# A vision tower on one core: attention four slots earlier, routing shared with GpSimd, and the chunk loop written out

## The reference, cut to what matters

```python
# 1: window attention, 8x8 windows, 8 heads of 8 channels, 2D rotary encoding
q, k, v = split(xw @ qkv_w.T + qkv_b);  q, k = rope2(q), rope2(k)
h = merge(softmax(q * 8**-0.5 @ k.T) @ v) @ proj_w.T + proj_b
# 2: mamba on layernorm(h), per image a scan over 4096 tokens
u = layernorm(h)
xb, z = split(rmsnorm(u) * norm_w @ in_proj_w.T)
xb = silu(causal_conv4(xb) + conv_b)                      # 128 channels
delta = softplus(xb @ projDelta_w.T + b);  B, C = xb @ projB_w.T, xb @ projC_w.T
state = exp(delta * A) * state + (xb * delta) * B         # 128 x 16 states
y = (sum(state * C) + xb * D) * silu(z)
h = h + y @ out_proj_w.T + u
# 3: experts on layernorm(h): 6 experts of three 64x64 layers, the best 2 of 6
p = softmax(relu(f @ rw1 + rb1) @ rw2 + rb2);  top2 = softmax(top_k(p, 2))
out = h + sum over top2 of weight * expert(f)
```

## Time and profile before

| | |
|---|---|
| median of 3 runs | 1921.03 us (1919.44 to 1929.98) |
| profiled execution | 1921.91 us, span 1920.1 us |
| PE busy | 1396.5 us (73%) |
| DVE busy | 1341.6 us (70%) |
| POOL busy | 1209.0 us (63%) |
| ACT busy | 1086.1 us (57%) |
| mean granted clock of TensorE | 0.806 |
| moved by DMA | 304.52 MB, mean 159 GB/s |
| first scan starts, last scan starts | 207.9 us, 1844.3 us |

### The profile page before, as it was taken

How to read it: one execution, slowest core, us unless ns; L and a number is a source line. 1 busy time by engine, 2 the same in 40 slices (tenths; PEclk the granted TensorE clock), 3 DMA queues, 4 the chain that set the end, 5 groups by cost and what they waited for, 6 DMA issues and landing times. The chain is left out here.

```text
span 1920.1 us, 31423 instructions
## 1 busy us (share of the span) xinstructions
PE 1396.5 (73%) x8148; PEld 648.9 (34%) x8148; DVE 1341.6 (70%) x1835; ACT 1086.1 (57%) x2020; POOL 1209.0 (63%) x1665
## 2 busy tenths in 40 slices
PE   3765768787969697786869687686868687666565
PEld 1443434343425243243424333242424333121111
DVE  1111688888786857878686867879686877878941
ACT  1234657675565747575475756566575857564432
POOL 2014486867685856767585765768586776967651
PEclk9877979796878878797788878796987978676755
DMA  2001686666565655666465665566566666777820
GB/s 63 1 14 57 162 226 192 195 187 173 159 200 156 182 167 157 189 186 173 138 185 174 165 190 162 174 169 193 150 170 184 172 198 175 213 192 204 222 70 6
DMA packets 214770, 304.52 MB, mean 159 GB/s; under 512 B 78924, under 2 KB 79128, under 8 KB 214424
## 3 DMA queue, kind: packets, MB, share of 16 engines
q1 hardware_dynamic: 214552, 302.09, 55.8%
HBM read 274.75 MB, written 20.97 MB: 154 GB/s over the span
## 5 line engine op out<-in xcount | busy, mean ns | idle before, releaser
L1262 POOL TENSOR_TENSOR hc<-hs,c_rep 128x512 f32<-128x512 f32 x512 | 652.2, 1274 | 461.0 <-DVE hs L1014 458.6
L1014 DVE TENSOR_TENSOR_SCAN hs<-bank,state,xd 128x512 f32<-128x512 f32 x512 | 650.8, 1273 | 83.2 <-issue 57.8
L767 ACT ACTIVATE bank<-dl,a_neg 128x512 f32<-128x512 f32 x512 | 350.3, 687 | 209.7 <-DVE hs L1014 186.7
L1005 DVE TENSOR_TENSOR xd<-xd,bank 128x512 f32<-128x512 f32 x512 | 337.1, 663 | 57.1 <-PE bank L439 53.3
L1032 DVE TENSOR_REDUCE neg_max<-bank 128x8 f32<-128x512 f32 x128 | 88.1, 688 | 281.1 <-PE bank L528 272.6
L538 PE MATMUL bank<-q_diag,k_heads 128*128 128x128 f32 x1024 | 226.4, 348 | 6.0 <-ACT shift L760 4.5
L538 PEld LDWEIGHTS bank<-q_diag,k_heads 128*128 128x128 f32 x1024 | 193.8, 229 | 82.8 <-issue 65.5
L775 ACT ACTIVATE probsT<-bank 128x512 f32<-128x512 f32 x128 | 76.4, 597 | 256.1 <-PE bank L539 255.6
L528 PE MATMUL bank<-k_heads,q_diag 128*128 128x512 f32 x256 | 175.1, 772 | 56.3 <-DMA q_diag<-rot 25.5
L449 PE MATMUL bank<-hc,wts 128*32 128x512 f32 x1024 | 182.8, 777 | 4.0 <-POOL hc L1262 2.6
L1334 POOL TENSOR_TENSOR ew<-ew,e 128x512 f32<-128x512 f32 x96 | 121.4, 1264 | 64.9 <-ACT e L760 64.8
(11 more groups left out here) (176 smaller groups left out, 2493.3 us busy)
## 6 DMA issues: line engine op xcount, KB each, us to landing
xd<-xdel_rows SPq DMA_DIRECT2D x512, 256.0 KB, 4.1
dl<-delta_rows SPq DMA_DIRECT2D x512, 256.0 KB, 3.8
delta_rows<-delta SPq DMA_DIRECT2D x16, 512.0 KB, 6.3
xdel_rows<-xdel SPq DMA_DIRECT2D x16, 512.0 KB, 3.1
xin<-in_x_dram SPq DMA_DIRECT2D x32, 128.0 KB, 2.4
q_diag<-rot SPq DMA_DIRECT2D x32, 128.0 KB
out_dram<-res SPq DMA_DIRECT2D x256, 16.0 KB
k_heads<-rot SPq DMA_DIRECT2D x128, 16.0 KB
```

What stands on the lines that cost most here:

```text
L767: act.activation(decay_ps[n % 2][:, :], dl[:, n % 4, :], ACT.Exp, scale=a_neg[:, g:g + 1])\
L1005: dve.tensor_tensor(xd[:, n % 8, :], xd[:, n % 8, :], b_ps[:, :], ALU.mult).then_inc(injected.sem, 1)
L1014: dve.tensor_tensor_scan(hs[:, n % 4, :], decay_ps[n % 2][:, :], xd[:, n % 8, :], state[:, g:g + 1], ALU.mult, ALU.add).then_inc(scanned.s ...
L1262: pool.tensor_tensor(hc[:, n % 8, :], hs[:, n % 4, :], c_rep[:, BAND * h:BAND * h + BAND], ALU.mult)\
```

## The change

`run` writes out all 21 bodies, and the counts become constants. Attention starts in slot 5 (`attention_at`), and `AT` gives the pairs 5, 6 and 7 three steps each; their maximum comes one step after their scores. What follows attention moves three slots ahead, as do SP's copies; the projection stands in slot 5 in a function of its own, and the sum of h and its layer norm moves from slot 6 of the next body to slot 17, in three buffers. `keys_queries` stands late in a slot. Of 26 routing steps 13 are on POOL, in slots 15 and 17 to 22, with DVE's in slots 15 and 17 to 22 and one memset dropped; the weights and all that follows move one slot back. `outT` shares its memory with `fT`. The matmuls of 8 columns are gone from `keys_queries` and `layer2`.

```diff
@@ -80,8 +80,8 @@
 
 
 
-AT = {"S": [9 + 2 * _w for _w in range(NW)], "max": [11 + 2 * _w for _w in range(NW)],
-      "T": [12 + 2 * _w for _w in range(NW)], "P": [13 + 2 * _w for _w in range(NW)]}
+AT = {"S": [9, 11, 13, 15, 17, 20, 23, 26], "max": [11, 13, 15, 17, 19, 21, 24, 27],
+      "T": [12, 14, 16, 18, 20, 23, 26, 29], "P": [13, 15, 17, 19, 21, 24, 27, 30]}
 
 
...
-        h_ln = sb("h_ln", [128, 2, NW, C])
+        h_ln = sb("h_ln", [128, 3, NW, C])
...
-        outT = sb("outT", [128, 512])
+
+        outT = fT
...
-        route_dve = sig("route_dve", 25)
+        route_dve = sig("route_dve", 12)
+        route_pool = sig("route_pool", 13)
...
@@ -284,18 +285,13 @@
         def attention_at(c, n):
 
 
-            return (c + 3, n - 9) if n >= 9 else (c + 2, n + 23)
+            return (c + 3, n - 5) if n >= 5 else (c + 2, n + 27)
 
         def run(eng, body):
 
 
 
-            for c in range(-3, 3):
-                body(c, c % 2)
-            with eng.Fori(3, NCH - 4, 2) as c:
-                body(c, 1)
-                body(c + 1, 0)
-            for c in range(NCH - 3, NCH + 2):
+            for c in range(-3, NCH + 2):
                 body(c, c % 2)
...
                     if has(c + 3):
-                        if n == 4:
+                        if n == 1:
                             load(c + 3)
-                        if 13 <= n < 15:
-                            heads(c + 3, 4 * (n - 13), 4 * (n - 12))
-                        if n == 14:
+                        if 10 <= n < 12:
+                            heads(c + 3, 4 * (n - 10), 4 * (n - 9))
+                        if n == 11:
                             queries(c + 3)
...
@@ -462,8 +458,6 @@
                     fill(use, k)
                 if names[0] == "k":
                     pe.wait_ge(A["xT"].drained, A["xT"].empty(k))
-
-                pe.matmul(uses[0].bank[0:32, 0:8], col("y_sel", 0, 32), xT[:, 0:8], start=True, stop=True)
                 for crossed, use in enumerate(uses):
                     for half in range(2):
                         p, to = slice(64 * half, 64 * half + 64), 64 * (half ^ crossed)
@@ -472,16 +466,16 @@
                     last.then_inc(use.filled, 1)
 
             def attend_first(k, s):
+                if s in AT["T"]:
+                    turned(k, AT["T"].index(s))
+                if s in AT["P"]:
+                    values(k, AT["P"].index(s))
+
+            def attend(k, s):
                 if s == 1:
                     keys_queries(k, ("k", "q"), ("wk", "wq"))
                 if s == 3:
                     keys_queries(k, ("k2", "q2"), ("wk2", "wq2"))
-                if s in AT["T"]:
-                    turned(k, AT["T"].index(s))
-                if s in AT["P"]:
-                    values(k, AT["P"].index(s))
-
-            def attend(k, s):
...
-                if s == 30:
+                if s == 31:
                     use = A["oT"]
                     fill(use, k)
                     pe.wait_ge(att_ready.sem, att_ready.at(k, 1))
...
-                if s == 31:
-                    use = A["proj"]
-                    fill(use, k)
+            def project(k):
+                use = A["proj"]
+                fill(use, k)
+                pe.wait_ge(A["oT"].drained, A["oT"].empty(k))
...
-                if n == 22:
+                if n == 23:
                     use = F["wT"]
                     fill(use, k)
-                    pe.wait_ge(route_dve.sem, route_dve.at(k, 25))
+                    pe.wait_ge(route_pool.sem, route_pool.at(k, 13))
...
-                if n == 25:
+                if n == 26:
                     use = F["outT"]
...
-                for e, slot in enumerate((27, 29, 31)):
+                for e, slot in enumerate((28, 30, 32)):
                     if n == slot:
                         layer3(k, e)
-                if n == SLOTS + 1:
+                if n == SLOTS + 2:
                     use = F["out"]
                     fill(use, k)
...
-                if 23 <= n < 23 + 2 * EP:
-                    j = PAIRED[n - 23]
+                if 24 <= n < 24 + 2 * EP:
+                    j = PAIRED[n - 24]
...
@@ -690,8 +684,6 @@
                 uses = F[f"h2_{e}"], G[f"h2_{e}"]
                 for use in uses:
                     fill(use, k)
-
-                pe.matmul(uses[0].bank[0:32, 0:8], col("y_sel", 0, 32), e1[:, 0, 0:8], start=True, stop=True)
...
@@ -722,6 +714,8 @@
                         spread_b(c + 1, 1 - odd, 0)
                     if has(k):
                         attend_first(k, s)
+                    if has(c + 2) and n == 5:
+                        project(c + 2)
...
-                if n == 15:
-                    act.wait_ge(route_dve.sem, route_dve.at(k, 3))
+                if n == 16:
+                    act.wait_ge(route_pool.sem, route_pool.at(k, 1))
                     act.activation(rt[:, 2, :, :], rt[:, 1, :, :], ACT.Exp).then_inc(route_act.sem, 1)
-                if n == 18:
-                    act.wait_ge(route_dve.sem, route_dve.at(k, 14))
+                if n == 21:
+                    act.wait_ge(route_pool.sem, route_pool.at(k, 6))
                     act.activation(st_f[:, 14, :], st_f[:, 13, :], ACT.Exp).then_inc(route_act.sem, 1)
...
-                if 24 <= n < 24 + 2 * EP:
-                    i = n - 24
+                if 25 <= n < 25 + 2 * EP:
+                    i = n - 25
...
-                if n == 22:
+                if n == 23:
                     use = F["wT"]
...
-                if n == SLOTS:
+                if n == SLOTS + 1:
                     use = F["outT"]
...
@@ -1033,7 +1027,7 @@
                                       X_AXIS, ALU.max, negate=True).then_inc(use.drained, 1)
 
             def attend(k, s):
...
-                if n == 9:
+                if n == 6:
                     use = A["proj"]
...
-                if n == 10:
+                if n == 7:
                     dve.wait_ge(A["proj"].drained, A["proj"].empty(k))
                     dve.tensor_reduce(st[:, 0, :], hid[:, :, :], X_AXIS, ALU.add).then_inc(done.sem, 1)
-                if n == 14:
+                if n == 11:
                     dve.wait_ge(ln1_act.sem, ln1_act.at(k, 1))
                     dve.tensor_reduce(st[:, 2, :], sq[:, :, :], X_AXIS, ALU.add).then_inc(done.sem, 1)
...
-                if 15 <= n < 20:
+                if 15 <= n < 23:
                     route(k, n)
...
@@ -1107,74 +1101,34 @@
             def route(k, n):
 
                 st, done = st_f, route_dve
+                def over(src, to, op):
+                    dve.tensor_reduce(st[:, to, :], rt[:, src, :, :], X_AXIS, op).then_inc(done.sem, 1)
+
                 if n == 15:
                     use = F["lg"]
                     dve.wait_ge(use.filled, use.full(k))
...
-                    dve.tensor_reduce(st[:, 10, :], rt[:, 0, :, :], X_AXIS, ALU.max).then_inc(done.sem, 1)
-                    dve.wait_ge(done.sem, done.at(k, 1))
-                    dve.tensor_tensor(rt[:, 1, :, :], rt[:, 0, :, :], wide_of(10), ALU.subtract).then_inc(done.sem, 1)
-                    dve.memset(rt[:, 12, :, :], 0.0).then_inc(done.sem, 1)
-                    dve.wait_ge(done.sem, done.at(k, 3))
-                if n == 16:
+                    over(0, 10, ALU.max)
+                if n == 17:
                     dve.wait_ge(route_act.sem, route_act.at(k, 1))
-                    dve.tensor_reduce(st[:, 11, :], rt[:, 2, :, :], X_AXIS, ALU.add).then_inc(done.sem, 1)
-                    dve.wait_ge(done.sem, done.at(k, 4))
+                    over(2, 11, ALU.add)
+                    dve.wait_ge(done.sem, done.at(k, 2))
                     dve.reciprocal(st[:, 12, :], st[:, 11, :]).then_inc(done.sem, 1)
-                    dve.wait_ge(done.sem, done.at(k, 5))
...
+
+                for i, (at, src, to, mask, count) in enumerate(((18, 3, 16, 4, 2), (19, 5, 10, 6, 3), (20, 7, 17, 8, 5),
+                                                                (21, 9, 10, 10, 7))):
+                    if n == at:
+                        dve.wait_ge(route_pool.sem, route_pool.at(k, count))
+                        over(src, to, ALU.max)
+                        dve.wait_ge(done.sem, done.at(k, 4 + 2 * i))
+                        dve.tensor_tensor(rt[:, mask, :, :], rt[:, src, :, :],
+                                          st[:, to, :].unsqueeze(2).to_broadcast([128, NW, E]), ALU.is_equal)                           .then_inc(done.sem, 1)
+                if n == 22:
+                    dve.wait_ge(route_pool.sem, route_pool.at(k, 8))
                     dve.reciprocal(st[:, 18, :], st[:, 15, :]).then_inc(done.sem, 1)
...
             def attend(k, s):
-                for at, i, names in ((4, 1, ("k", "k2")), (4, 0, ("q", "q2"))):
+                for at, i, names in ((5, 1, ("k", "k2")), (5, 0, ("q", "q2"))):
                     if s == at:
...
-                if n == 11:
+                if n == 8:
```

(51 more changed lines are left out.)

121 lines of the change are left out of this document (41 added, 80 removed).

## The result

The changed kernel takes 1966.95 us (median of 4 runs, 1950.07 to 1978.08), the kernel before beside it 1923.74 (1919.44 to 1929.98): ratio 1.0215, 95% interval 1.0132 to 1.0297, so it is slower, and whether by more than 2% is open. Forecast were 1840 (1775 to 1905).

A forecast was written before the change was run, and what follows sets the result against it. No single engine bounds the body: DVE and ACT bound B, DVE and POOL C, PE D. Per body +3 + 4 - 11 - 0.7 = -4.7, -56 over bodies 1 to 12; with the loop's -25, -81: 1840 us (1775 to 1905).

The forecast's parts named there:

- The loop, -25: Bodies 3 to 12: writing out the rounds removes the stalls at four loop returns, 25 us in all.
- Stretch D: Slot 23 to slot 3 of the next body, bound by PE: less attention and shorter score waits, -11 us per body.
- Prologue: Before the first scan: one more attention window, but its first two stages end sooner by as much; 0 (-4 to +6).
- Stretch B: Slot 4 to the first routing step of slot 15: earlier attention work moves in, +3 us per body (0 to +6).
- The routing, in a C at +4: From slot 15's routing to scan 23: half the routing to POOL, two more attention windows; +4 us per body.
- My marker: DVE's new waits for POOL's steps sum to under 2 us a body; at 5 or more the forecast is wrong.
- The other marker: The forecast is also wrong if bodies 3 to 12, written out straight, still last 106 us.
- Rival (c): Slots 18 to 22: DVE held to POOL, 6.3 us per body, total 1934; decides from 5.4 on; chance 0.11.
- Small matmuls: Five tiny two-pass matmuls per chunk are dropped: at most 1.4 us, taken as -0.7 us per body.
- (b): D falls to DVE's own work, C stays: -184 and the loop, 1712; half of it called 1770; chance 0.12.
- (a): PE and ACT stay in step with the half clock, C gives back D's gain, only the loop counts: 1896; chance 0.16.

The follow-up runs named there:

- e1: Kernel before, with its rounds written out and nothing else changed; 1888.99 us, ratio 0.969-0.992.
- e8: Changed kernel with only the scores of pairs 5, 6 and 7 moved one, two and two steps ahead; 1884.94 us, ratio 0.971-0.997.
- e2: e1 plus 13 routing steps on POOL and what follows them one slot later, attention as before; 1842.42 us, ratio 0.941-0.961.
- e9: e8 with keys and queries at the head of their slots again; 1875.48 us, ratio 0.970-0.990.
- e5: e2 without the 8-column matmuls; 1835.19 us, ratio 0.949-0.969.
- e10: e8 with attention and all that follows it four slots later, starting in slot 9; 1936.28 us, ratio 1.002-1.027.
- e12: Changed kernel with two slots per pair, attention from slot 9, keys and queries at the head of their slots; 1935.76 us, ratio 0.998-1.024.
- e3: Changed kernel with the routing on DVE in slots 15 to 19 as before; 2037.67 us, ratio 1.050-1.066.
- e6: Changed kernel with the 8-column matmuls put back; 1998.13 us, ratio 1.023-1.052.
- e13: e5 with only the layer norm behind attention one slot later on DVE, ACT and POOL; 1858.95 us, ratio 0.967-0.988.
- e15: e5 with the sum of h and its layer norm on POOL in slot 21, three buffers, outT in fT's memory; 1903.48 us, no ratio.
- e16: e9 with the rotation's second pair, POOL's adds, ACT's key heads and SP's copies one slot earlier; 1938.84 us, ratio 1.008-1.040.

## Why the prediction was wrong

**The loop, -25: right in kind, low.** e1 measures -38; ten bodies at 105.8 save 31. One premise did not hold: the bodies that meet no return were not all like body 3 (bodies 4, 6 and 8 took 108.7, 112.0 and 108.7 us), so the spread of the bodies is not the returns' alone.

**Stretch D, -11: the step that failed.** I counted what leaves D (7.2 us; the product is 7.1) and added a third of the waits, and took "one slot apart instead of two" for a remainder. It is the main term. A pair is a chain: scores, maximum, shift, turned block, exponential, values. With two slots between score and maximum two pairs overlap. With one slot, and S behind T in one PE queue, they do not: PE's idle time in D rose from 1.9 to 8.0 us while the maxima went on waiting for PE. Waits for scores stayed at 13.0 a body (13.4 before), 12.0 of them in D, where I had about 7 left of all waits, and D shrank by 5.1. e8 moves these three scores and nothing else: 82 us, most of the 127 by which the forecast missed.

**Prologue, 0 (-4 to +6): +25.** The same chain, where nothing covers it. I priced the window that goes further ahead and not the spacing. How much of the 25 is the chain is known only roughly, since two kernels with the same code up to there (e1, e2) start their first scan at 199.3 and 214.2. Bodies 0 to 2 lost 24 more where I had -9.

**Stretch B, +3 (0 to +6): +6.0, mis-sized.** That is twice the term and the upper end of its range. DVE waits 4.48 us for keys that stand behind z, and 4.28 for a softplus behind ACT's copies of v and key heads: work I had seen in the queues and hidden. e9 suggests that the two are one: what the rotation gains the softplus loses, 7.7 us a body together in e8 and 7.5 in e9. Between e8 (1885) and e5 (1835) lie 3.3 us a body: 7.6 less of these waits in e5 and 4.6 more for scores. e10 to e12 forbid calling it the price of the start slot as such: with the start in slot 9 and late keys the rotation waits 7.1 and 5.3 us.

**The routing, in a C at +4: about right for C, wrong for the split.** C grew by 2.5. Cut at scan 15 and against e1, it is 1.9 us longer with the split alone (e2), 2.2 with the attention alone (e3) and 3.8 with both. So DVE's gain does not show in C, as I had said, but I let it end there, and the split gives -47 in all, in D (e2). Why D gains, beyond the clock's part, is not shown. My marker, 5 us or more of waits for POOL, came true (7.0 after), and it was a bad marker: e2 shows 7.6 and gains. I read it so that such a wait takes the place of one for scores that would have come later; the rows show only that the one sum rose while the other fell. The other marker, straight bodies that still last 106, came true as well: they last 110.5. Rival (c) had its place and its size (it decides from 5.4 us on) and was still not the cause. The 3.02 us before the reciprocal are not even POOL's: its step waits 5.06 us for an exponential that stands on ACT behind two expert layers and the exp of a turned block, for which ACT waits 2.16 us for PE.

The Trainium skill, "SBUF — State Buffer", section "Who interferes with whom", says that a DVE instruction with two SBUF inputs contends with a GpSimd instruction that reads SBUF. The comparison L1127 agrees: 0.23 us in one slot of e12, beside POOL steps of 0.20, and 1.02 in the next, beside one of 1.27, on the same shape. What this carried of the time no run shows; four such steps remained, in a stretch where DVE waits for POOL anyway.

**Small matmuls, -0.7 a body: not told in one kernel, low in the other.** The -7 of e5 would be -0.6 a body and lies within the spread; the 31 of e6 are 2.6 a body over 12.

**Rivals.** None was it. Half of (b)'s -184, with the loop, is 1804 and not 1770. (a) put the gain of D into C's clock; C's clock was 0.92. What came true is a rival I did not write: the new schedule's own chain of dependences.

**What stays open.** How much of e13, e15 and e16 is the edit and how much is the clock that it meets in D. The rows show the first delay in e15, 0.67 us, and later bodies that are 6 us longer; between them stands the clock, and no run here moves the one without the other. The same holds for e2. Why e12 takes 100 us more than e5 is only partly explained: its layer norm costs 24 alone, its sum 38 to 43 alone. Its bodies are 8.6 us longer, with 3.4 us more of waits for scores, 3.2 for the rotation and 1.6 for POOL; that names the places and not the cause. In e8, the distance of score and maximum and their order behind the turned blocks changed together.

## What to carry to other kernels

When work is spread over more slots, check the distance between producer and consumer of each link, not only the work that leaves a full stretch: one or two slots less between score and maximum cost 82 us, as much as the whole edit was to bring (81). A prologue without cover shows that chain first, in a few rows of spacing. Split a combined edit before judging it: here the loop and the routing together took 4% off (e5, ratio 0.959), and the rest of the change lost 132 us over that.
